# Loading and splitting ten of sixteen expert weight parts inside the attention before the mixture

## What is computed

```python
def _L0_ffn_ref(x, wg1, bg1, wg2, w_in, w_out):      # E, H, K, G = 8, 512, 2, 64
    g = gelu(xt @ wg1 + bg1)
    top_vals, top_idx = top_k(softmax(g @ wg2), K)
    h = gelu(einsum('nd,edh->enh', xt, w_in))
    y = einsum('ne,end->nd', gates, einsum('enh,ehd->end', h, w_out))
x = x + _L0_xattn_ref(_layernorm(x), ctx_768, ...)
x = x + _L0_ffn_ref(_layernorm(x), ...)
x = x + _L1_xattn_ref(_layernorm(x), ctx_768, ...)
x = x + _L1_ffn_ref(_layernorm(x), ...)
```

## Time and profile before

| | us |
|---|---|
| three runs | 1029.51, 1034.25, 1035.13 |
| median | 1034.25 |
| profiled execution, its own time | 1031.65 |
| span in that execution | 1029.8 |
| attention A ends (last sum into X) | 485.3 |
| mixture: first expert transpose on TensorE | 550.2 |

### The profile page before, as it was taken

One profiled execution on the slowest core, in us unless ns is written; L12 is line 12 of the kernel. 1 busy time (PEld: TensorE's weight loads), 2 busy tenths in 40 slices (PEclk: granted clock), 3 DMA queues, 4 the chain that ended last, 5 costly groups with the idle time before them and its releaser, 6 DMA issues. The chain is left out here.

```text
span 1029.8 us, 23468 instructions
## 1 busy us (share of the span) xinstructions
PE 831.7 (81%) x8808; PEld 507.9 (49%) x8808; DVE 755.0 (73%) x1515; ACT 711.9 (69%) x1183; POOL 624.1 (61%) x574
## 2 busy tenths in 40 slices
PE   4876999999999999977525999868788979961576
PEld 4533565556555656554223777523445555651243
DVE  5858888788878886774685555458989887728796
ACT  3387999899979998961542444336897979924674
POOL 2078677777777777851345666424787878924142
PEclk9999999999999999996557999977999999966798
DMA  8579999999999999990964889762999979953155
GB/s 252 192 135 174 157 177 181 181 167 179 184 179 168 171 175 170 174 174 3 247 243 98 183 186 186 144 235 51 182 195 179 187 141 184 184 98 128 37 113 133
DMA packets 504878, 167.96 MB, mean 163 GB/s; under 512 B 477728, under 2 KB 495328, under 8 KB 504736
## 3 DMA queue, kind: packets, MB, share of 16 engines
q1 hardware_dynamic: 501024, 156.25, 81.4%
q0 software_dynamic: 3744, 10.23, 3.5%
HBM read 37.04 MB, written 11.14 MB: 47 GB/s over the span
## 5 line engine op out<-in xcount | busy, mean ns | idle before, releaser
L475 POOL TENSOR_TENSOR A_PHL<-A_pr,A_PHL 128x508 f16<-128x508 f32 x256 | 293.7, 1153 | 93.7 <-ACT A_pr L755 93.3
L754 ACT ACTIVATE A_PHL<-A_ps,A_negmax 128x508 f16<-128x508 f32 x256 | 190.1, 743 | 16.4 <-DVE A_negmax L999 13.3
L755 ACT ACTIVATE A_pr<-A_ps,A_negmax 128x508 f32<-128x508 f32 x256 | 191.8, 749 | 0.0
L475 POOL TENSOR_TENSOR C_PHL<-C_pr,C_PHL 128x512 f16<-128x512 f32 x128 | 149.6, 1178 | 51.2 <-ACT C_pr L755 51.1
L999 DVE TENSOR_REDUCE A_negmax<-A_ps 128x2 f32<-128x1016 f32 x128 | 154.2, 1205 | 0.0
L600 PE MATMUL A_ps<-A_K,A_Q 64*128 64x512 f16 x768 | 106.6, 383 | 18.0 <-ACT A_pr L755 13.9
L618 PE MATMUL A_ps<-A_VH,A_PT 128*128 128x65 bf16 (+1 forms) x1024 | 107.2, 195 | 7.8 <-DMA A_PT<-A_PHL 7.8
L619 PE MATMUL A_ps<-A_VL,A_PT 128*128 128x64 f16 (+1 forms) x1024 | 107.1, 193 | 0.0
L620 PE MATMUL A_ps<-A_VH,A_PT 128*128 128x65 bf16 (+1 forms) x1024 | 107.0, 194 | 0.0
L618 PEld LDWEIGHTS A_ps<-A_VH,A_PT 128*128 128x128 f16 (+1 forms) x1024 | 94.4, 98 | 22.1 <-DMA A_PT<-A_PHL 11.1
L754 ACT ACTIVATE C_PHL<-C_ps,C_negmax 128x512 f16<-128x512 f32 x128 | 90.8, 709 | 18.1 <-DVE C_negmax L999 17.3
(11 more groups left out here) (344 smaller groups left out, 2317.1 us busy)
## 6 DMA issues: line engine op xcount, KB each, us to landing
A_PT<-A_PHL SPq DMA_TRANSPOSE x256, 3.4
M_raw<-in_L_ffn_w_in SPq DMA_DIRECT2D x4, 1024.0 KB, 8.3
M_raw<-in_L_ffn_w_out SPq DMA_DIRECT2D x4, 1024.0 KB, 8.7
C_yc<-routed_rows SPq DMA_DIRECT2D x8, 512.0 KB, 5.0
M_rows<-M_xhl SPq DMA_DIRECT2D x4, 512.0 KB, 9.1
out<-X SPq DMA_DIRECT2D x16, 128.0 KB, 2.0
X<-in_x SPq DMA_DIRECT2D x1, 1536.0 KB, 14.1
ct_split<-A_CT SPq DMA_DIRECT2D x4, 384.0 KB, 2.8
```

The lines of the kernel that those rows point to most:

```text
L475: pool.tensor_tensor(PHL[:, e % PRING, 1, 0:KEYS], pr[:, e % RING, 0:KEYS], PHL[:, e % PRING, 0, 0:KEYS], ALU.subtract).then_inc(pl_ready. ...
L754: a.activation(PHL[:, e % PRING, 0, 0:KEYS], o, ACT.Exp, bias=nm[:, n % 4, h:h + 1])
L755: a.activation(pr[:, e % RING, 0:KEYS], o, ACT.Exp, bias=nm[:, n % 4, h:h + 1]).then_inc(p_ready.sem, 1)
```

## The change

Parts 0 to 9 (w_in and w_out of experts 0 to 4) are loaded inside attention A, one DMA of 512 KB each on SP's queue, behind the transposes of steps 33, 35, 45, 49, 61, 75, 79, 91, 95 and 109. Each part is split in two halves of 512 columns, the high half by ScalarE and the low one by GpSimd, at the end of steps u = 9, 11, 13, 15, 25, 27, 29 of blocks 1 to 3 (20 halves). The weights lie in memory that the attention's low-rank and projection weights used at its start, for which the attention's other tensors go to the other side of SBUF; the last three experts' place is used until the attention's end, and their six parts stay in the front: two loads of 1.5 MB, one behind the fourth row transpose and one behind the eighth. ScalarE makes their six high parts, VectorE their six low parts (two after `choose(1)`, one before the counts, three behind the table); GpSimd splits nothing in the front.

```diff
+class ExpertWeights:
+    E, H, PARTS, EARLY = 8, 512, 16, 10
...
+    def load(self, sp, k):
+        which, e = self.part(k)
+        if k >= 2:
+            sp.wait_ge(self.split, 2 * (k - 1))
+        src = self.source(which, e)
+        sp.dma_start(self.raw[:, k % 2, :].rearrange("p (c n) -> p c n", n=src.shape[2]), src).then_inc(self.loaded[k % 2], 16)
...
+    def half_high(self, a, j):
+        raw, hi, lo = self.half(j)
+        a.wait_ge(self.loaded[j // 2 % 2], 16 * (j // 4 + 1))
+        a.activation(hi, raw, ACT.Copy).then_inc(self.hi, 1)
+
+    def half_low(self, pool, j):
+        raw, hi, lo = self.half(j)
+        pool.wait_ge(self.hi, j + 1)
+        pool.tensor_tensor(lo, raw, hi, ALU.subtract).then_inc(self.split, 1)
...
+    def load_rest(self, sp, which, rest):
+        n = (self.PARTS - self.EARLY) // 2
+        src = self.w[("w_in", "w_out")[which]][self.EARLY // 2:self.E]
+        sp.dma_start(rest[:, which * n:(which + 1) * n, :].rearrange("p e (c n) -> p e c n", n=src.shape[3]),
+                     src.rearrange("e p c n -> p e c n")).then_inc(self.rest_loaded[which], 16)
...
 def attention(...):
+    HALF_AT = [b * U + u for b in range(1, B) for u in (9, 11, 13, 15, 25, 27, 29)][:2 * nxt.EARLY] if nxt else []
+    LOAD_AT = {HALF_AT[max(2 * k - 3, 0)] + (2 if k > 1 else 2 * k - 8): k for k in range(nxt.EARLY)} if nxt else {}
...
+            return within.enter_context(nc.sbuf_tensor(f"{tag}_{name}", shape, dt, side="right" if nxt and within is ctx else "left"))
...
+        if nxt:
+            first_out.close()
+            nxt.place()
+            nxt.raw = sb("wraw", [P, 2, nxt.E * P], F32)
...
                 if ipa and u == 18 and b:
                     wait(sp, pj_filled, JOB["y", b - 1, 2 * QT - 1] + 1)
                     load_vwo(b)
+                if n in LOAD_AT:
+                    nxt.load(sp, LOAD_AT[n])
...
+                if n in HALF_AT:
+                    nxt.half_low(pool, HALF_AT.index(n))
...
+                if g in HALF_AT:
+                    nxt.half_high(a, HALF_AT.index(g))
...
 def mixture(...):
-            load_w(0)
-            turn_rows(0)
-            turn_rows(1)
-            load_w(1)
-            turn_rows(2)
-            turn_rows(3)
-            load_w(2)
+            for p in range(4):
+                turn_rows(p)
+            weights.load_rest(sp, 0, raw)
             for p in range(4, PAIRS):
                 turn_rows(p)
-            load_w(3)
+            weights.load_rest(sp, 1, raw)
             for b in range(B):
                 store_rows(b)
-            for k in range(4, len(LOADS)):
-                load_w(k)
...
-            pool.wait_ge(rows_split, PAIRS)
-            for k in BY_POOL:
-                W, e = PARTS[k]
-                pool.wait_ge(w_hi, k + 1)
-                pool.tensor_tensor(W[1][:, e, :, :].rearrange("p c n -> p (c n)"), raw[:, k % RAWS, :],
-                                   W[0][:, e, :, :].rearrange("p c n -> p (c n)"), ALU.subtract).then_inc(w_split, 1)
...
+            for b in range(B):
+                gate_gelu(b)
+                if b:
+                    weights.high(a, weights.EARLY + b - 1, raw)
+            for k in range(weights.EARLY + B - 1, weights.PARTS):
+                weights.high(a, k, raw)
...
             choose(0)
-            w_low(0, 4)
             choose(1)
-            w_low(4, 6)
+            weights.low(v, 10, raw)
+            weights.low(v, 11, raw)
...
-            w_low(6, 8)
+            weights.low(v, 12, raw)
...
-            w_low(8, 2 * E)
+            for k in range(13, weights.PARTS):
+                weights.low(v, k, raw)
```

More of the change, by code:

```diff
@@ L135, in layernorm_stats, with __init__, place, sem @@
     return stat, rest, act
-def attention(nc, tag, X, ident, identh, stats, w, ctx_t, heads, ipa, scratch, x_in=None, routed=None):
+class ExpertWeights:
+    E, H, PARTS, EARLY = 8, 512, 16, 10
+    def __init__(self, nc, tag, stats, w):
+        self.nc, self.tag, self.stats, self.w = nc, tag, stats, w
+        self.room = ExitStack()
+    def place(self):
+        def sem(name):
+            return self.stats["scope"].enter_context(self.nc.semaphore(f"{self.tag}_{name}"))
+        E, H = self.E, self.H
+        W = self.room.enter_context(self.nc.sbuf_tensor(f"{self.tag}_W", [P, E, 4, KC * H], F16))
+        self.kinds = [W[:, :, n, :] if n % 2 == 0 else W[:, :, n, :].bitcast(BF16) for n in range(4)]
+        self.WIN = [w.rearrange("p e (c n) -> p e c n", n=H) for w in self.kinds[0:2]]
+        self.WOUT = [w.rearrange("p e (c n) -> p e c n", n=D) for w in self.kinds[2:4]]
+        self.loaded = [sem(f"w_loaded{k}") for k in range(2)]
+        self.rest_loaded = [sem(f"w_rest_loaded{k}") for k in range(2)]
+        self.hi, self.split, self.split_v = sem("w_hi"), sem("w_split"), sem("w_split_v")
+    def part(self, k):
+        if k < self.EARLY:
+            return k % 2, k // 2
+        n = self.PARTS - self.EARLY
+        return (k - self.EARLY) // (n // 2), self.EARLY // 2 + (k - self.EARLY) % (n // 2)
+    def source(self, which, e):
+        return self.w[("w_in", "w_out")[which]][e]
+    def load(self, sp, k):
[4 more added lines that the diff above has]
+        sp.dma_start(self.raw[:, k % 2, :].rearrange("p (c n) -> p c n", n=src.shape[2]), src).then_inc(self.loaded[k % 2], 16)
+    def half(self, j):
+        which, e = self.part(j // 2)
+        c = slice(j % 2 * self.H, (j % 2 + 1) * self.H)
+        return self.raw[:, j // 2 % 2, c], self.kinds[2 * which][:, e, c], self.kinds[2 * which + 1][:, e, c]
+    def half_high(self, a, j):
[11 more added lines that the diff above has]
+                     src.rearrange("e p c n -> p e c n")).then_inc(self.rest_loaded[which], 16)
+    def high(self, a, k, rest):
+        which, e = self.part(k)
+        a.wait_ge(self.rest_loaded[which], 16)
+        a.activation(self.kinds[2 * which][:, e, :], rest[:, k - self.EARLY, :], ACT.Copy).then_inc(self.hi, 1)
+    def low(self, v, k, rest):
+        which, e = self.part(k)
+        v.wait_ge(self.hi, 2 * self.EARLY + k - self.EARLY + 1)
+        v.tensor_tensor(self.kinds[2 * which + 1][:, e, :], rest[:, k - self.EARLY, :], self.kinds[2 * which][:, e, :],
+                        ALU.subtract).then_inc(self.split_v, 1)
@@ L140, in attention @@
+def attention(nc, tag, X, ident, identh, stats, w, ctx_t, heads, ipa, scratch, x_in=None, routed=None, nxt=None):
     HD = heads * DH
@@ L1039, in _, with mixture @@
                     v.tensor_tensor(o, o, bcast(mi[:, :], IPA), ALU.mult).then_inc(ipa_p.sem, 1)
-def mixture(nc, tag, X, identh, stats, w, routed):
+def mixture(nc, tag, X, identh, stats, w, routed, weights):
     E, H, G = 8, 512, 64
@@ L1064, in mixture @@
         dst_u = sb("dst_u", [P, NT], U32)
[L1066 to L1068 removed]
+        WIN, WOUT = weights.WIN, weights.WOUT
+        raw = sb("raw", [P, weights.PARTS - weights.EARLY, KC * H], F32)
         xn = sb("xn", [P, TILES, D], F32)
@@ L1342, in _ @@
             pe.wait_ge(table_ready, 3)
-            pe.wait_ge(w_split, lows(2 * E, True))
-            pe.wait_ge(w_split_v, lows(2 * E, False))
+            pe.wait_ge(weights.split, 2 * weights.EARLY)
+            pe.wait_ge(weights.split_v, weights.PARTS - weights.EARLY)
             expert = {}
@@ L1394, in _ @@
         def _(a):
-            def w_high(first, last):
-                for k in range(first, last):
-                    W, e = PARTS[k]
-                    a.wait_ge(w_loaded[k // PAIR % SETS], 16 * (k // PAIR // SETS + 1))
-                    a.activation(W[0][:, e, :, :].rearrange("p c n -> p (c n)"), raw[:, k % RAWS, :], ACT.Copy).then_inc(w_hi, 1)
             def row_high(p):
@@ L1478, in choose @@
                 return last
-            def w_low(first, last):
-                for k in range(first, last):
-                    if k in BY_POOL:
-                        continue
-                    W, e = PARTS[k]
-                    v.wait_ge(w_hi, k + 1)
-                    v.tensor_tensor(W[1][:, e, :, :].rearrange("p c n -> p (c n)"), raw[:, k % RAWS, :],
-                                    W[0][:, e, :, :].rearrange("p c n -> p (c n)"), ALU.subtract).then_inc(w_split_v, 1)
             one, two, half_v = spare_k
```

77 lines of the change are left out of this document (20 added, 57 removed).

## The result

The changed kernel took **1038.06 us** (median of 13 runs, 1033.55 to 1044.52), the kernel before beside it 1029.51 (13 runs, 1020.59 to 1036.36). The ratio is 1.0093, 95% interval 1.0068 to 1.0117: slower by 0.9% (the two medians alone stand 8.55 us, 0.83%, apart). A timing of the same size on another chip gave 1.0099 (1.0059 to 1.0138), a smaller one of four runs 1.014. The forecast was 1028.2 with a range of 1021 to 1037, so both sign and range were wrong. The profiled execution took 1042.96 us (span 1041.2).

What follows compares the result with a forecast made beforehand. TensorE was taken to set the attention's pace, ScalarE close behind, with a nearly full transpose queue; the front was a chain. Costs 4 + 0.5 minus gain 10.5 made -6.0 us: 1034.25 to 1028.2 us, range 1021 to 1037.

Steps and rivals of the forecast that it cites:

- Table and last splits: Mixture's front: VectorE's table instructions no longer stretched by GpSimd's splits, 7.4 us gained; three last splits instead of four, 1.2 us.
- Gate: Mixture's front: less weight data ahead of the row transposes, so gate product three starts earlier, gaining 1.9 us (0.5 to 2.5).
- ScalarE: Attention: twenty 512-column copies mostly fit ScalarE's idle time; 0.5 us leaks at three places, at worst 12 us.
- GpSimd: Attention: twenty splits of 1.15 us fit into GpSimd's 68.2 us of idle time; cost nothing, at most 1 us.
- Sync queue: Attention, the deciding term: ten loads at 1.35 us each delay the weight transposes; TensorE stalls, 4 us together.
- account: Attention: loads' delay followed through the transposes, using up 13.3 us of queue waits for GpSimd; 2.9 us stall at 1.35 each.
- rival 2: Attention: each load passes on its whole transit of 2.0 us; 7.7 us of stall, total 1032 us; chance 0.2.
- the subtraction of 0.7: Sync queue: a load's 2.0 us cut to 1.35, since hold-ups come anyway and two in three loads should miss one.
- (1): Attention: the queue absorbs the loads, only 0.64 us of issue counts; attention costs 0.5 to 1, total 1024.5 us; chance 0.2.
- (3): Attention: each load costs 3.3 us by making hold-ups longer, TensorE stalls 19 us, total 1043 us; chance 0.1.
- (4): Front: the split stays on the path (row stores late, or gate gain nil); 2 to 3 us less gain; no separate chance.

Runs made afterwards that it cites:

- r_before: The kernel before, unchanged, profiled a third time on one chip with the changed kernel; attention steps 396.6 us.
- r_after: The changed kernel, unchanged, profiled a third time on one chip with the kernel before; attention steps 415.7 us.
- e3_halves: Against e1_place: the twenty copies and splits added at their places, with only two loads; steps 408.4 us, ratio 1.0113 to the kernel before.
- e7_halves_moved: Against e3_halves: copies and splits moved, none in steps 11 to 15 of blocks 1 and 2, two loads moved too; steps 399.3 us, ratio 0.9972.
- e4_actq: Against the changed kernel: its ten loads issued by ScalarE's queue, one step later; steps 415.7 us, ratio 1.008 to the kernel before.
- e2_loads: Against e1_place: the ten 512 KB loads added on the sync queue, nothing splits them; steps 409.5 us, ratio 1.011 to the kernel before.
- e1_place: Changed kernel's memory layout alone, without loads, copies or splits inside the attention, front of the kernel before; steps 397.0 us, ratio 1.0038.
- e0_after: The changed kernel once more, unchanged, in four runs; steps 417.6 us, ratio 1.014 to the kernel before.
- c_before: The kernel before, unchanged, profiled again on another chip; steps 396.6 us, first maximum at 54.9 us.

## Why the prediction failed, point by point

The front over all profiles, from the attention's end to the last choice (COPY M_L) and from there to the first expert transpose. The rows of r_before and of r_after:

```profile
487.37 0.42 DVE L880 TENSOR_TENSOR X<-A_ps,X 128x256 f32<-128x256 f32 x1 [1.62 <-PE A_ps L585]
...
519.34 0.17 DVE L1470 COPY M_L<-M_ps 128x32 f32<-128x32 f32 x1
...
550.68 0.39 PE L1356 MATMUL M_ps<-identh,M_xg 128*128 128x128 f16 x2 [7.13 <-DVE M_WOUTl L1486]
```
```profile
501.58 0.42 DVE L968 TENSOR_TENSOR X<-A_ps,X 128x256 f32<-128x256 f32 x1 [1.62 <-PE A_ps L671]
...
534.70 0.19 DVE L1501 COPY M_L<-M_ps 128x32 f32<-128x32 f32 x1 [0.43 <-PE M_ps L1360]
...
557.42 0.39 PE L1404 MATMUL M_ps<-identh,M_xg 128*128 128x128 f16 x2 [5.99 <-DVE M_W L206]
```

| us | before (three profiles) | after (four) | gain | predicted |
|---|---|---|---|---|
| end of attention to last choice | 33.3, 31.4, 31.5 | 31.4, 32.8, 32.7, 32.6 | -0.3 | 1.9 |
| last choice to first expert transpose | 31.3, 31.2, 31.3 | 22.7, 22.7, 22.7, 22.8 | 8.5 | 8.6 |
| steps of the attention | 398.9, 396.6, 396.6 | 414.9, 417.6, 415.7, 411.4 | -17.5 | -4.5 |

- **Table and last splits: right** to 0.1 us, from the stretched rows 7 and 8 and the splits of rows 3.
- **Gate: mis-sized**, 1.9 predicted, nothing measured. The profile of before, on which the term rested, has the longest of its three gates. And the load of 1.5 MB landed 7.9 us after its issue (it was issued at 517.79), not 6.9: 5.5 was the least of eight landings on an empty queue, and 1.4 us for the further half MB was not enough. The transposes behind it came later too, and gate product three waited 3.64 us for them.
- **ScalarE: right.** At steps 9, 25, 27 and 29, and anywhere in block 3, copy and split together lengthened no step of e3_halves; with all twenty moved, they and the splits cost 0.5 us together from step 25 on (e7_halves_moved).
- **GpSimd: wrong, and the largest miss.** "Nothing, at most 1 us" was in truth some 9 us. The step that failed is the sentence that GpSimd idles 68.2 us and that its inputs come late enough. It asked only who waits for GpSimd. It didn't ask who runs well *because* GpSimd is idle. The very same effect, VectorE's instructions stretched beside splits, carried the front's largest term, seen in rows 7 and 8, and block 0 of the same attention shows it too; the work was moved to a place where it does the same. No rival held this mechanism.
- **Sync queue: mechanism right, price and account too small.** The price was taken as 1.35 and is 1.96: rival 2's value. Its reason is not: with the loads on ScalarE's ring (e4_actq) no ring order stands between load and transpose, and the price is the same. The step that failed is the subtraction of 0.7, two in three loads missing a hold-up; ten in ten had one. (Hold-ups are also rarer than the "some ten times per 100 us" of the text: 25 transposes over 1.5 us in 300.) But rival 2 put 7.7 us of stall beside its price, and e2_loads lost 12.5. Two things stand in the rows for the remaining 4.8. The transposes behind each load land 1.6 us later after their issue, for which the account put 0.4 at three places. And the account let the queue spend its idle time in full, yet of the 12.5 us only 4.4 had come by step 96 and 8.1 come behind it, where a single load lies and two more (steps 91 and 95) just ahead; 2.4 of them are the wait at step 126 that the first profile of before has as well. How the 4.8 divide between the two, no run shows.
- **The other rivals.** (1) fell with the first load. (3), 3.3 us a load, fell too, though its size for the total, 1043, came nearest: the right total by a wrong mechanism. (4) came true in one half: the gate gained nothing, within the size that it named.
- **The layout: right** to give it nothing; unpriced in the text, it costs 0 in the steps (397.0 and 396.7 against 397.4). The ratio of e1_place, 1.0038 with an interval just above 1, is not accounted for by its rows.
- **The total.** -17.5 + 8.2, and 1.4 us of difference between last step and end of the attention that lies within its spread, make 10.7 us slower. Measured: 0.93 and 0.99%, 9.6 and 10.3 us (the medians stand 8.6 and 8.4 apart); the four runs of e0_after gave 1.4%.
- What "would show it": the stalls were expected behind steps 34, 36 and 62 and none in steps 9 to 15. They lay at 35, 51, 62, 65, 93 and at the end of block 3; and steps 12 to 16 were just where the other half of the loss sat.

## What to carry to other kernels

An idle engine is not free time as long as another engine is held up by its work: before you fill GpSimd's holes, look for VectorE's instructions that run in them, with two inputs above all and however small, and read their duration beside GpSimd's work; if they stretch in one stage, they will in the next. In a queue that is full, charge a transfer its issue and its transit at every place, read how much later the transfers behind it land, and follow the debt to the end of the stage before you call it absorbed. And read a term from more than one execution where it is small: the start and the gate here vary by 8 and 2 us in executions of one kernel.

## What the runs showed of the hardware

- A plain load of 512 KB between transposes holds up one of the two behind it: the second at all ten loads of the changed kernel (1.85 to 3.65 us for 1.33), the first at two of ten in e2_loads (2.91 and 2.19). From another engine's queue it does so as well (2.40 in e4_actq).
- The two transposes behind such a load land 5.1 us after their issue, where the median is 3.5; the first lands after the load, ten of ten, from either queue.
- A VectorE instruction of four columns, 0.16 us, takes 1.08 to 1.12 us beside a GpSimd split of 1.15, and ends with it.
- In one and the same kernel the first maximum stands at 60 to 62 or at 53 to 55 us, and from 8 to 28 us the loads move less or more: the kernel before 250 to 306 GB/s, the changed one 223 to 314.
- In c_before the first to the last rise of M_hf lie 128.0 us apart, where the profile of before has 105.3; seven waits of ScalarE there, of up to 7.8 us (row below), have a releaser that the trace doesn't name. It goes by the chip: on three of them every kernel has 119 to 128 us for this stretch, on the others 105 to 108. The cause is open; it is in both sides of each ratio.

```profile
ACT M_hf L1436 <- remote: 49.1, 7, 7.8
```
